# A pre-norm decoder layer on one core: the convolution on 16-bit halves, one eight-term sum on VectorE, and the rows of the two last batches weighted in the feed-forward stage

## What is computed

```python
x = x + attention(layernorm(x))        # 32 heads, 8 key groups, rope, alibi, tanh cap, causal
x = x + xattn(ctx, ctx, layernorm(x))
x = x + ffn(layernorm(x))              # ternary weights, silu gate, rms norm

# xattn, with k = v = ctx, H = 32 heads of 8 rows, length L = 512
kv  = einsum('bhil,bhjl->bijhl', k_, v_)
y   = irfft(rfft(kv, 2 * L) * rfft(ssm_kernel, 2 * L))[..., :L]   # causal convolution along L
out = y + kv * D
out = einsum('bijhl,bhil->bjhl', out, q_)
```

## Time and profile before

| | |
|---|---|
| median of three runs | 1182.75 us |
| span of the profiled execution | 1182.6 us |
| TensorE busy | 1146.9 us, 97% |
| VectorE busy | 877.6 us, 74% |
| GpSimd busy | 688.9 us, 58% |
| ScalarE busy | 554.0 us, 47% |
| granted TensorE clock, mean | 0.995 |

### The profile page before, as it was taken

How to read it: one execution, slowest core, us unless ns; L and a number is a source line. 1 busy time by engine, 2 the same in 40 slices (tenths; PEclk the granted TensorE clock), 3 DMA queues, 4 the chain that set the end, 5 groups by cost and what they waited for, 6 DMA issues and landing times. The chain is left out here.

```text
span 1182.6 us, 24878 instructions
## 1 busy us (share of the span) xinstructions
PE 1146.9 (97%) x9715; PEld 794.2 (67%) x9730; DVE 877.6 (74%) x1287; ACT 554.0 (47%) x617; POOL 688.9 (58%) x557
## 2 busy tenths in 40 slices
PE   4888999999999999999999999999999999999998
PEld 4655556657657566566565677777886776786683
DVE  6879878787888787878887688889745745654654
ACT  6766565564755656647556400000244543542441
POOL 1454395784865957849659589999342422423331
PEclk9999999999999999999999999999999999999999
DMA  9563443554445335543455367772012022012000
GB/s 324 156 201 116 121 131 111 164 188 117 125 146 173 122 123 167 187 120 120 129 174 186 116 124 148 143 150 67 1 20 48 7 55 54 18 35 54 19 19 36
DMA packets 166142, 133.48 MB, mean 113 GB/s; under 512 B 69628, under 2 KB 127362, under 8 KB 166082
## 3 DMA queue, kind: packets, MB, share of 16 engines
q1 hardware_dynamic: 141128, 126.44, 36.3%
q10 hardware_dynamic: 24960, 6.29, 3.6%
HBM read 81.76 MB, written 35.21 MB: 99 GB/s over the span
## 5 line engine op out<-in xcount | busy, mean ns | idle before, releaser
L700 PE MATMUL bank<-hT_halves,w_hi 128*128 128x256 f16 x640 | 176.2, 275 | 5.4 <-DVE hT_halves L1419 3.6
L1973 POOL TENSOR_TENSOR parts<-parts 128x512 f32<-128x512 f32 x80 | 118.8, 1489 | 106.8 <-DVE parts L1435 106.8
L701 PE MATMUL bank<-hT_halves,w_hi 128*128 128x256 f16 x640 | 175.8, 275 | 0.0
L702 PE MATMUL bank<-hT_halves,w_lo 128*128 128x256 f16 x640 | 175.8, 275 | 0.0
L952 PE MATMUL bank<-kv,toep 128*128 128x288 f32 (+2 forms) x660 | 159.5, 404 | 0.7 <-ACT qT L1200 0.5
L1978 POOL TENSOR_SCALAR_AFFINE_SELECT region_c<-region_c 128x512 f32<-128x512 f32 x128 | 113.2, 908 | 63.5 <-ACT region_c L1166 63.3
L952 PEld LDWEIGHTS bank<-kv,toep 128*128 128x128 f32 x660 | 124.7, 192 | 34.4 <-ACT qT L1200 0.8
L2121 POOL TENSOR_TENSOR sqsum<-sqsum,toep 128x512 f32<-128x512 f32 x56 | 78.0, 1393 | 95.5 <-ACT toep L1342 95.3
L1991 POOL TENSOR_TENSOR ctx_lo<-ctx,ctx_hi 128x512 f16<-128x512 f32 x64 | 99.0, 1547 | 59.1 <-ACT ctx_hi L1142 59.1
L1163 ACT ACTIVATE region_c<-bank,cap_scale 128x1536 f32<-128x1536 f32 x64 | 98.7, 1542 | 74.2 <-PE bank L768 73.6
L1031 PE MATMUL bank<-odd_halves,guT 128*128 128x256 f16 x512 | 112.2, 273 | 0.0
(11 more groups left out here) (192 smaller groups left out, 2666.4 us busy)
## 6 DMA issues: line engine op xcount, KB each, us to landing
unit_halves<-halves SPq DMA_DIRECT2D x80, 256.0 KB, 2.2
q_both<-unit_halves SPq DMA_DIRECT2D x64, 256.0 KB, 2.9
q_high<-unit_halves SPq DMA_DIRECT2D x64, 128.0 KB, 3.0
toep<-kernel_padded SPq DMA_DIRECT2D x32, 256.0 KB, 3.9
wffn<-w_gu SPq DMA_DIRECT2D x6, 1280.0 KB, 6.2
cpair<-ctx_pairs SPq DMA_DIRECT2D x32, 176.0 KB, 4.8
xin<-x SPq DMA_DIRECT2D x8, 512.0 KB, 3.9
region_o<-wq SPq DMA_DIRECT2D x4, 1024.0 KB, 11.3
```

The source lines that it names most:

```text
L700: pe.matmul(dst, lh, rh, start=first and k == 0, stop=False)
L701: pe.matmul(dst, lh, rl, start=False, stop=False)
L702: mm = pe.matmul(dst, ll, rh, start=False, stop=last and k == n - 1)
L1973: pool.tensor_tensor(slot[:, 0], slot[:, 0], slot[:, 1], ALU.add).then_inc(unit_summed, 1)
```

## The change

Convolution. Context pairs are scaled to a fixed range (ScalarE, `scale_pairs`). ScalarE makes the eight squares of a pair set, GpSimd the other products. ScalarE rounds `kv` to fp16 (`high_kv`), and GpSimd makes the low half (`low_kv`). The convolution kernel is likewise stored as two fp16 halves. TensorE takes three fp16 products in place of one fp32 product. `halve` is gone, and `gather` sums eight terms. VectorE weights only batches 0 to 5 (`KEEP = 6`), 24 columns out of 32. ScalarE copies y of batches 6 and 7 out of PSUM (`keep_y`), SyncE stores it to HBM (`store_late`).

Scales. The largest row square of the context (eight loads of 512 KB into `xin`, squared by ScalarE during attention) and of the kernel have to be known before the first pair can be scaled. They go through HBM once (`tops_d`) to reach all partitions, and VectorE works out the scales in the last batch (`find_conv_scales`). The halves of the kernel are stored after that, and the loads of `cpair` and `toep` follow them in SyncE's queue.

Feed-forward. In batches 0 to 3, at each of the eight steps, GpSimd weights one head of the two late batches (`weigh_late`), and VectorE sums it (`gather_late`) one step later; SyncE loads y and x of that head (`load_late`), two heads ahead. SyncE issues the transposes of the ternary weights now: eight during the convolution, four after it. The feed-forward loops are written out.

```diff
                     for m in range(l + 1):
-                        d = l - m
-                        mm = pe.matmul(dst, toep[:, n, d * P:(d + 1) * P], kv[:, p, m * B + batches.start:m * B + batches.stop, :],
-                                       start=(m == 0), stop=(m == l))
+                        block = slice((l - m) * P, (l - m + 1) * P)
+                        hi, lo = [kvh[:, p, v, m * B + batches.start:m * B + batches.stop, :] for v in range(2)]
+                        pe.matmul(dst, toep[:, n, 0, block], hi, start=(m == 0), stop=False)
+                        pe.matmul(dst, toep[:, n, 0, block], lo, start=False, stop=False)
+                        mm = pe.matmul(dst, toep[:, n, 1, block], hi, start=False, stop=(m == l))
...
+            def freed(h):
+                pe.wait_ge(y_free, h - 1)
+                pe.wait_ge(y_kept, h - 1)
...
+            def prepare_kv(h, n):
+                pool.wait_ge(pair_scaled, h + 4)
+                pool.wait_ge(kv_lo_done, h + 2)
+                products((n + 3) % AHEAD)
+                low_kv(h + 2, n % 2)
...
+            def low_kv(h, p):
+                pool.wait_ge(kv_hi_done, h + 1)
+                pool.tensor_tensor(kvh[:, p, 1], kv[:, p], kvh[:, p, 0], ALU.subtract).then_inc(kv_lo_done, 1)
...
+            def serve(h, n, q):
+                high_kv(h + 2, n % 2, True)
+                square_kv(h + 3, (n + 3) % AHEAD, True)
+                scale_pairs(h + 4, n, q + 1)
+                keep_y(h, n % 2, AHEAD // 2 * q + n // 2)
...
             def mix(h, p, first=False):
-                dve.wait_ge(y_filled, h + 1)
-                mix_behind(h, p, slice(0, LB * B))
                 if not first:
                     dve.wait_ge(mix_done, h)
-                mix_ahead(h, p, slice(0, LB * B)).then_inc(y_free, 1)
+                dve.wait_ge(y_filled, h + 1)
+                mix_behind(h, p, every)
+                mix_ahead(h, p, every).then_inc(y_free, 1)
...
+                if step == 0:
+                    square_ctx(b - 1)
+                if step == 2:
+                    square_ctx(b)
...
+            def weigh_late(h):
+                p = h % 2
+                pool.wait_ge(late_in[p], 32 * (h // 2 + 1))
+                if h >= 2:
+                    pool.wait_ge(late_done, h - 1)
...
+            def gather_late(h):
+                dve.wait_ge(late_mixed, h + 1)
+                dve.tensor_reduce(outT[:, :, KEEP:B, h, :], windows(late_slots[h % 2].rearrange("p (c x) -> p c x", x=HD * HD), 0, [[1, HD], [HD, HD]]),
                                  AX_X, ALU.add).then_inc(late_done, 1)
...
+                    if b < LATE_FFN and n:
+                        gather_late(HB // 2 * b + n - 1)
...
+            def turn_weights(n):
+                if n:
+                    sp.wait_ge(tern_in, 16 * n)
...
+            for h in range(2):
+                load_late(h)
...
+            for n in range(GU_TURNS, TURNS):
+                turn_weights(n)
+            load_late_behind(0)
+            sp.wait_ge(tern_in, 16 * TURNS)
```

More of the change, by code:

```diff
@@ L126, in decoder_layer @@
         exponent = sb("exponent", [P, 1])
+        conv_scales = sb("conv_scales", [P, CHUNKS + 11])
+        ctx_squares, rest = conv_scales[:, 0:CHUNKS], conv_scales[:, CHUNKS:]
+        tops, c_top, c_root, c_inverse = [rest[:, 2 * n:2 * n + 2] for n in range(4)]
+        pair_scale, t_scale, y_undo = [rest[:, n:n + 1] for n in range(8, 11)]
         with ExitStack() as p1:
@@ new lines, in follow @@
+            def follow(n, h):
+                sp.wait_ge(y_filled, h + 1)
+                if h < HM - AHEAD:
+                    load_toep(h + AHEAD, n)
+                if h < HM - AHEAD - 2:
+                    sp.wait_ge(kv_ready, h + 3)
+                    sp.wait_ge(kv_squared, h + 3)
+                    load_pairs(h + AHEAD + 2, (n + 2) % AHEAD)
+                store_late(h)
+            sp.wait_ge(quant_stored, QUANT_STORES * (SHARES - 1) + FIRST_QUANT_STORES)
+            for h in range(HM - 1):
+                follow(h % AHEAD, h)
+                if h == X2_LAST_BEHIND + 2:
+                    sp.wait_ge(qT_free, B * TT)
+                    sp.dma_start(q_late_d, q_late[:].rearrange("p h l b r -> p h (l b r)")).then_inc(conv_moved, 16)
+                if h % 3 == 0 and h // 3 < GU_TURNS:
+                    turn_weights(h // 3)
@@ L1219, in last_batch @@
                 high_ctx(b, NG - 1, False)
+                for h in range(2):
+                    scale_pairs(h, h)
+                    square_kv(h, h)
+                for h in range(2, AHEAD):
+                    scale_pairs(h, h)
                 for g in range(STEPS - WO_AFTER, NG):
@@ L1222, in last_batch @@
                         take_x2(n)
[L1223 to L1224 removed]
+                    if g >= NG - 2:
+                        high_kv(g - (NG - 2), g % 2)
             def sum_rows(n):
@@ L1382, in _ @@
             act.activation(first_silu[:], ident_s[:, 0:1], ACT.Silu)
+            keep_y(HM - 1, 1, HM // 2 - 1)
             act.wait_ge(y_free, HM)
+            act.wait_ge(conv_moved, 80)
             ffn(0, 0, first=True)
-            ffn(1, 1)
-            with act.Fori(1, B // 2 - 1) as i:
-                ffn(2 * i, 0)
-                ffn(2 * i + 1, 1)
-            ffn(B - 2, 0)
-            ffn(B - 1, 1, last=True)
+            for b in range(1, B):
+                ffn(b, b % 2, last=b == B - 1)
             for q in range(4):
@@ L2044, in last_batch @@
                     low_ctx(b, g)
-                for n in range(NG + 4 - STEPS):
-                    pool.wait_ge(toep_in[n], 32)
-                    products(n)
+                for h in range(2):
+                    pool.wait_ge(pair_scaled, h + 1)
+                    products(h)
+                    low_kv(h, h)
+                pool.wait_ge(pair_scaled, 3)
+                pool.wait_ge(kv_lo_done, 1)
+                products(2)
                 deviation(B + 1, 4 * (B * TT), ln2_mv, ln2_var, ln2_rstd, rest)
```

444 lines of the change are left out of this document (300 added, 144 removed).

## The result

The changed kernel takes 1270.09 us, median, against 1182.75. The ratio, 1.0727 (95% interval 1.0708 to 1.0747), is that of the fast runs alone, 1269.06 to 1270.70 us; the median is over four runs, and the fourth took 1453.41 us at a mean granted clock of 0.793. The forecast was 1262 with a range of 1202 to 1288. The profiled execution has a span of 1267.3 us, 84.7 more than before.

The account below looks back on a forecast made before the run. TensorE was taken to bound the kernel, VectorE 0.5 us behind it. 1182.6 + 13.7 (entry) + 5.9 (convolution) + 1 (hand-over) + 29 (batch 0) + 30 (batches 1 to 3) = 1262 us; range 1202 to 1288.

Parts of the forecast that it names:

- What bounds: Convolution: VectorE replaces TensorE as the bound, 5.07 us a head against 4.85; +5.9 us over 27 heads.
- The rule on reductions: Convolution's eight-term sum: skill's table gives one element per cycle whatever the stride; forecast instead priced by L1807, 3.03 us.
- The entry: Start to head 3's first multiplication: context squares and scales delay the convolution; +13.7 us, ends +5 and +25.
- two trips through HBM, 3 us each, so to 661: Entry into the convolution: after ternary stores end at 655, the scales' data takes two trips, estimated 3 us each.
- Batch 0: Feed-forward batch 0: four transposes, 7.7 us each to land, delay late head 2 and the fifth gate; +29 us.
- Batches 1 to 3: Feed-forward batches 1 to 3: late sums lengthen middle steps and delay standardising; 10 us per batch, +30 us.
- a step of 4.6 us: Feed-forward batches 1 to 3, middle steps: VectorE's 3.47 us plus 1.1 for a late sum, against TensorE's 3.5.
- stalls for late heads: Feed-forward batches 1 to 3: stalls of some 4 us ahead of the standardising's end, beside eight sums of 9 us.
- rival 1: Feed-forward batches 0 to 3: late work hides in VectorE's waits, losing about 8 us together; total 1211, chance 0.18.
- Rival 2: Convolution: eight-term sum takes 1.8 us, GpSimd's 4.25 becomes the bound; -16 us, total 1240, chance 0.09.
- Rival 3: Convolution: TensorE's clock halves in half the heads, 30 products taking 7.2 us; +29 us, total 1291, chance 0.07.
- Rival 4: Convolution: three half-rate products for one don't shorten TensorE, 7.3 us a head; 1262 + 60 = 1322, chance 0.01.

Follow-up runs that it names:

- Run 5: Changed kernel with the convolution's eight-term sum adding eight adjacent products instead of eight lying eight apart (not the terms that belong together): 1247.5 us.
- Run 1: Changed kernel with all twelve transposes of the ternary weights issued during the convolution, one every second head, none behind it: 1258.4 us.
- run 10: Changed kernel without any late work in the feed-forward stage (no loads, weighting or sums of late heads; their rows set to zero once): 1220.8 us.
- run 8: Changed kernel, all transposes in the convolution, last ternary store behind scales' trips, context squares in steps 2 and 3, late heads mostly under down products: 1226.7 us.
- run 9: Changed kernel with the last ternary store behind the scales' two HBM trips, and those trips ahead of the two reloads of x: 1266.8 us.
- run 2: Changed kernel with the last share of ternary weights stored behind the scales' two HBM trips and the first `toep` load: 1268.3 us.

## Why the prediction was right, point by point

**What bounds.** Right: VectorE took over as the bound of the convolution, at 5.05 us a head for a forecast of 5.07. The sum took 2.95 where I took 3.03 between 2.83 and 3.23. The wait for the own sum took 0.23, where the earlier trace rows gave 0.15; the four multiplications 1.87. The two small errors cancel. +5.3 us for +5.9.

**The rule on reductions.** The tier table of the Trainium skill (VectorE: DVE Perf Modes, The perf-mode tier table) would have had the sum at one element per cycle. Run 5 measures 1.13 ns an element for adjacent terms and 1.92 for terms 32 bytes apart, in one kernel with one line changed: the table agrees with the first alone. What the Trainium skill (SBUF — State Buffer, Specifications) says of a penalty for each new 16-byte line agrees with both.

**The entry: the right places, undersized.** Forecast 13.7, measured 24.9, at the end of my range. The term that failed is "two trips through HBM, 3 us each, so to 661". The load of the second trip landed at 670.8: 4.1 us of the difference are that the store was issued at 659.1 and not at 655, behind the ternary stores, and 5.8 that it took 8.8 us and not 3. It stood behind reloads of 3.5 MB that I didn't have in the sum, though their issue is a row of SyncE's list before as well:

```profile
639.75 1.17 SPq L641 DMA_DIRECT2D x2r<-x_scratch  x2
```

And I hadn't named what is queued behind VectorE's wait: attention's normalisation. From the scales to the first convolution 25.6 us passed where I had 26, but that is luck, since the path isn't mine. The chain that ended last goes from VectorE's scales through the rest of attention on TensorE (672.8 on) and ScalarE's copies of the turned x (`qT`, L1383, 682.5 on) to the first set's halves, and not through the store of the kernel's halves and the loads behind it. The context's load took 5.9 us (614.55 to 620.46) in place of 3.9.

**Batch 0: the right wait, at a wrong price.** Forecast 29, measured 15.8. Four transposes take 14.8 us and not 4 + 3 x 7.7: I had priced them by their landing on ScalarE's queue in the convolution, and took the bound of 4 us only for the range. Run 1 gives what they cost, 7.8. The other 8 us have a part that I had at nothing, the last two sums in front of the second gated step. In the changed kernel these end at 881.9, far ahead of the third late sum at 898.3, so that they lie under its wait; they show when the transposes are gone (run 1) or all late work is (run 10).

**Batches 1 to 3: right mechanism, one term missing.** Forecast 30, measured 37.9. I had a step of 4.6 us; in batch 2 the four are 5.2, 4.9, 5.8 and 5.8, and 2.5 of the 3.3 us above my price are the multiplication, lengthened by the contention between VectorE's and GpSimd's operations, which no term of mine had. The stalls for late heads, which I had at some 4 us, are 7.7. That I took every operation at its price alone, while the change puts GpSimd to work beside VectorE's most loaded steps, is the general error. Run 10 shows that the late work is the whole loss there: without it the three periods are 126.3 us, as before. Behind the gaps that it makes on TensorE the clock falls, to 0.96 in the mean with 9.5 us more of busy time; no run tells how much of that the kernel's time shows.

**The rivals.** That late rows hide (rival 1) is false as the change orders them; run 8 shows that most of it hangs on the order: the three periods are 9.1 us above the 126.3 of before, and batch 4 is 4.3 above its 42.2. Rival 2 is false for the change, whose sum takes 2.95 us; run 5 shows what it would have given. Rival 3 is half false: the clock stays at 1.00 in the convolution's 27 heads, with TensorE busy some 3.9 of 5.05 us; but it does fall where TensorE has longer gaps, to a mean of 0.90 from 600 us to head 3 and 0.89 in batch 0, and over the span it is 0.977 instead of 0.995. Rival 4 is false: 0.12 us a product. So the total was near partly by luck, since errors of +11, -13 and +8 partly cancel; the convolution's part was right by itself.

## What to carry to other kernels

A gain on the engine that sets the pace is worth only the distance to the next engine: here TensorE had about 1 us a head less to do, VectorE stood 0.5 us behind it, and work was added there. Work moved to "idle" time of another stage has to be placed in the idle stretches of its engines' lists; spread evenly over the steps it lengthened batches 1 to 3 by 38 us, and by 9, with 4 more in batch 4, once it lay mostly under the down products (run 8). For every wait that a change adds, look at what is queued behind it on its engine, and for every small transfer on a critical path, at the large ones issued just before it.

## What was not expected of the hardware

- VectorE's multiplication of two operands in SBUF and GpSimd's products slow each other: 1.22 us becomes 2.27, and 0.26 becomes 1.24. The one that starts second lengthens. The late sums, which have one operand, take 1.05 to 1.11 us with and without GpSimd at work. That agrees with the Trainium skill (SBUF — State Buffer, Who interferes with whom), which has a VectorE instruction with two SBUF inputs contend with a GpSimd instruction that reads SBUF, and one with a single input not.
- A store of 1 KB landed after 3.6 us issued ahead of 3.5 MB of loads (run 9), after 13.5 right behind them (run 2), and after 8.8 issued 9 us behind them with the last ternary stores between (the changed kernel).
- The same four DMA transposes landed after 7.7 us (median) issued by ScalarE in the convolution before, after 4.3 issued by SyncE in the convolution of run 1, and after 4.1 issued by SyncE in the changed kernel's feed-forward stage. The DMA engines were about as busy in the first two cases (a share of 0.73 between 763 and 797 us, of 0.70 between 787 and 822), so a busy stretch isn't the reason. What differs is the engine that issues them; why that matters, no run here shows.
